# Second feed-forward of a two-layer model: a tile's rows turned by VectorE in 32x32 blocks, after a load in four parts, in place of a turn on TensorE

## The reference

```python
xn = rms_norm(x, norm_scale)
scores = einsum('bsd,ed->bse', xn, w_router)
_, ids = top_k(scores, 2)
c = take_along_axis(softmax(scores), ids)
h = einsum('bsd,ehd->bseh', xn, w_up)
val, gate = split(h, 2)
h = val * silu(gate)
y = einsum('bseh,edh->bsed', h, w_down)
out = sum(take_along_axis(y, ids) * c) + skip
```

## Time and profile before

| | us |
|---|---|
| median of 3 runs | 2190.05 (2188.83 to 2192.83) |
| profiled execution, span from first to last instruction | 2242.6 |
| PE busy over the span | 1743.5 (78%) |
| DVE busy | 1650.1 (74%) |
| ACT busy | 1349.8 (60%) |
| POOL busy | 1185.3 (53%) |

### The profile page before, as it was taken

One profiled execution on the slowest core, in us unless ns is written; L12 is line 12 of the kernel. 1 busy time (PEld: TensorE's weight loads), 2 busy tenths in 40 slices (PEclk: granted clock), 3 DMA queues, 4 the chain that ended last, 5 costly groups with the idle time before them and its releaser, 6 DMA issues. The chain is left out here.

```text
span 2242.6 us, 44681 instructions
## 1 busy us (share of the span) xinstructions
PE 1743.5 (78%) x13783; PEld 1370.5 (61%) x13783; DVE 1650.1 (74%) x4953; ACT 1349.8 (60%) x3266; POOL 1185.3 (53%) x1272
## 2 busy tenths in 40 slices
PE   5688999899976656949994777777777651999994
PEld 5577777777753442426662555555566541999993
DVE  7599999999966982438986999999755432555554
ACT  4577777777744993228772788888444331556551
POOL 3277777877740004842314788888724455444440
PEclk8699999999986756969997999999865555999997
DMA  3000000000013112341200000000220111222217
GB/s 112 12 2 2 2 2 2 2 2 2 2 52 121 39 39 56 48 113 57 66 10 1 1 1 1 1 1 1 78 106 30 34 38 57 70 66 64 66 51 230
DMA packets 103368, 92.05 MB, mean 41 GB/s; under 512 B 11696, under 2 KB 93744, under 8 KB 102432
## 3 DMA queue, kind: packets, MB, share of 16 engines
q1 hardware_dynamic: 80128, 62.77, 9.1%
q0 software_dynamic: 14560, 22.24, 3.8%
q10 hardware_dynamic: 8448, 4.20, 0.6%
HBM read 46.26 MB, written 42.91 MB: 40 GB/s over the span
## 5 line engine op out<-in xcount | busy, mean ns | idle before, releaser
L2263 POOL TENSOR_TENSOR delta_A<-delta_A,delta_sW 128x256 f32<-128x256 f32 x256 | 193.4, 755 | 78.9 <-ACT delta_sW L2110 52.8
L2033 PE MATMUL delta_u<-delta_m,tables_sb 128*128 128x256 f32 x512 | 166.3, 407 | 82.1 <-DVE delta_m L2183 82.1
L2883 POOL DMA_INDIRECT choice_rows<-ffn_y,ffn_xg x135 | 128.7, 953 | 170.8 <-DVE ffn_y L2990 165.6
L644 ACT ACTIVATE attn_p_att<-attn_score,attn_mx 128x224 f32<-128x224 f32 (+7 forms) x512 | 146.6, 394 | 102.3 <-DVE attn_mx L735 102.3
L630 ACT ACTIVATE attn_p_geo<-attn_kp_wide,attn_geo_cols 128x32 f32<-128x32 f32 (+6 forms) x448 | 179.0, 482 | 2.5
L573 PE MATMUL attn_score<-attn_k,attn_q_diag 128*128 128x64 f32 (+5 forms) x1024 | 177.8, 317 | 0.0
L2110 ACT ACTIVATE delta_sW<-delta_W,tables_sb 128x256 f32<-128x256 f32 x256 | 126.6, 506 | 79.6 <-DVE delta_W L2205 75.8
L2033 PEld LDWEIGHTS delta_u<-delta_m,tables_sb 128*128 128x128 f32 x512 | 87.2, 190 | 132.4 <-DVE delta_m L2183 125.7
L2029 PE MATMUL delta_u<-delta_v_own,tables_sb 128*128 128x256 f32 x512 | 153.6, 382 | 9.6 <-DVE xnT L2170 9.6
L2840 POOL DMA_INDIRECT rows<-mix_rows,mix_slot x128 | 124.6, 973 | 56.8 <-issue 52.5
L573 PEld LDWEIGHTS attn_score<-attn_k,attn_q_diag 128*128 128x128 f32 x1024 | 149.5, 193 | 7.3
(11 more groups left out here) (401 smaller groups left out, 5044.8 us busy)
## 6 DMA issues: line engine op xcount, KB each, us to landing
ffn_xg<-rows SPq DMA_DIRECT2D x135, 66.0 KB
acc<-route_zero SPq DMA_DIRECT2D x10, 832.0 KB
comb_rows<-choice_rows SPq DMA_DIRECT2D x32, 256.0 KB
rows<-route_rows SPq DMA_DIRECT2D x8, 640.0 KB, 3.4
load_rows<-in_x SPq DMA_DIRECT2D x16, 256.0 KB, 4.9
bT<-acc SPq DMA_DIRECT2D x16, 256.0 KB, 4.1
qT<-acc SPq DMA_DIRECT2D x16, 256.0 KB, 4.9
x_kept<-xT SPq DMA_DIRECT2D x16, 256.0 KB, 2.1
```

Of the source, the lines that this page charges most:

```text
L644: last = nc.scalar.activation(p_att[:, gr, PAIR_OFF[n]:PAIR_OFF[n] + SLOT * (n + 1)], score[at][:, c:c + SLOT * (n + 1)], ACT.Exp, bias=mx ...
L2033: nc.tensor.matmul(corrections(h, pp % 2), g.t("same_head"), m1[:, h].rearrange("p t d b -> p (t d b)"), start=False, stop=True).then_inc( ...
L2263: nc.gpsimd.tensor_tensor(A[:, t % 8], A[:, (t - 1) % 8], sW[:, t % RING], ALU.add).then_inc(k.A, 1)
L2883: nc.gpsimd.indirect_dma_start(g.choice_rows, bass.IndirectOffsetOnAxis(xg[:, n % RING, D:D + 1].bitcast(U32), 0), y[:, n % RING, :], None ...
```

## The change

SP loads a tile's rows with five transfers. Four bring the channels in four blocks of 32: the transfer for block i puts, for each of the four groups of 32 rows, row b of the group on partition 32 i + b. The fifth brings the last four words of all rows into a tile of its own, `tail`. Then DVE turns within each 32x32 block, and `xgT` has what PE's turn and ACT's copy gave: channel on the partition, row in the free dimension. The turn on PE, its PSUM banks and the copy on ACT are gone. `turn` stands in DVE's list where the loop brings the val weights for tile n+2, ahead of the product of tile n and the weighting of tile n-2. POOL and the weighting read number and share from `tail`.

```diff
+    LOADS = D // SLOT + 1
...
-        xg = s.sb("xg", [128, RING, ROW1])
+        xg = s.sb("xg", [128, RING, D // SLOT, SLOT])
+        tail = s.sb("tail", [128, RING, ROW1 - D])
...
-                sp.dma_start(xg[:, n % RING, :], g.rows1[bass.ds(row, 128), :]).then_inc(ring[n % RING].loaded, 16)
+                here = g.rows1[bass.ds(row, 128), :]
+                by_slot = here[:, 0:D].rearrange("(j b) (i a) -> b i j a", b=SLOT, a=SLOT)
+                for i in range(D // SLOT):
+                    sp.dma_start(xg[SLOT * i:SLOT * i + SLOT, n % RING], by_slot[:, i]).then_inc(ring[n % RING].loaded, 16)
+                sp.dma_start(tail[:, n % RING, :], here[:, D:ROW1]).then_inc(ring[n % RING].loaded, 16)
...
-            def turn(n):
-                par = n % 2
-                pe.wait_ge(ring[n % RING].loaded, 16 * (n // RING + 1))
-                if n >= 2:
-                    pe.wait_ge(k[par].x_copied, n // 2)
-                nc.tensor.transpose(x_ps[par][:, 0:128], xg[:, n % RING, 0:D], g.t("ident")).then_inc(k[par].turned, 1)
-
             def up(n):
                 par = n % 2
-                pe.wait_ge(k[par].x_copied, n // 2 + 1)
+                pe.wait_ge(k[par].turned, n // 2 + 1)
...
-            def copy_x(n):
-                par = n % 2
-                act.wait_ge(k[par].turned, n // 2 + 1)
-                if n >= 4:
-                    act.wait_ge(k[par].val, n // 2 - 1)
-                nc.scalar.activation(xgT[:, n % 4, :], x_ps[par][:, 0:128], ACT.Copy).then_inc(k[par].x_copied, 1)
-
...
+            def turn(n):
+                par = n % 2
+                dve.wait_ge(ring[n % RING].loaded, LOADS * 16 * (n // RING + 1))
+                if n >= 4:
+                    dve.wait_ge(k[par].val, n // 2 - 1)
+                nc.vector.transpose(xgT[:, n % 4, :], xg[:, n % RING].rearrange("p j a -> p (j a)")).then_inc(k[par].turned, 1)
...
             for n in range(AHEAD):
                 bring_val(n)
+                turn(n)
             for n in range(TILES1 + BEHIND):
                 if n + AHEAD < TILES1:
                     bring_val(n + AHEAD)
+                    turn(n + AHEAD)
                 if n < TILES1:
                     hidden(n)
                 if n >= BEHIND:
```

More of the change, by code:

```diff
@@ L2864, in ffn_phase @@
         hid = s.sb("hid", [128, 4, WIDE])
-        x_ps, val_ps, gate_ps, y_ps = ([s.ps(f"{n}{par}") for par in range(2)] for n in ("x", "val", "gate", "y"))
+        val_ps, gate_ps, y_ps = ([s.ps(f"{n}{par}") for par in range(2)] for n in ("val", "gate", "y"))
         ring = [s.sems("loaded sent", n) for n in range(RING)]
         padded = s.sems("padded").padded
-        k = [s.sems("w_val w_gate turned x_copied gate val sg hid down y", par) for par in range(2)]
+        k = [s.sems("w_val w_gate turned gate val sg hid down y", par) for par in range(2)]
         block = s.block()
@@ L2882, in _ @@
                 pool.wait_ge(k[n % 2].y, n // 2 + 1)
-                nc.gpsimd.indirect_dma_start(g.choice_rows, bass.IndirectOffsetOnAxis(xg[:, n % RING, D:D + 1].bitcast(U32), 0),
+                nc.gpsimd.indirect_dma_start(g.choice_rows, bass.IndirectOffsetOnAxis(tail[:, n % RING, 0:1].bitcast(U32), 0),
                                              y[:, n % RING, :], None).then_inc(ring[n % RING].sent, 16)
@@ L2922, in _ @@
             pe.wait_ge(padded, 1)
-            for n in range(AHEAD):
-                turn(n)
             for n in range(TILES1 + BEHIND):
-                if n + AHEAD < TILES1:
-                    turn(n + AHEAD)
                 if n < TILES1:
@@ L2957, in _ @@
                 bring_gate(n)
-                copy_x(n)
             for n in range(TILES1):
@@ L2961, in _ @@
                     bring_gate(n + AHEAD)
-                    copy_x(n + AHEAD)
                 silu(n)
@@ L2989, in output @@
                     dve.wait_ge(ring[n % RING].sent, 16 * (n // RING))
-                nc.vector.tensor_scalar(y[:, n % RING, :], y_ps[par][:, 0:D], xg[:, n % RING, D + 1:D + 2], None, ALU.mult)\
+                nc.vector.tensor_scalar(y[:, n % RING, :], y_ps[par][:, 0:D], tail[:, n % RING, 1:2], None, ALU.mult)\
                     .then_inc(k[par].y, 1)
```

## The result

| | us |
|---|---|
| kernel before, median of 4 runs | 2190.83 (2188.83 to 2192.83) |
| changed kernel, median of 4 runs | 2350.47 (2348.71 to 2351.05) |
| ratio | 1.0727, 95% interval 1.0714 to 1.0740 |
| profiled execution of the changed kernel, span | 2349.2 |

What follows compares the result with a forecast made beforehand. SP's queue was to replace PE as the bound: 135 tiles at 3.40 us, 459 us, put the profiled combine start 171 us later; less profiling overhead, between 2341 and 2361, it took 2348 us, range 2280 to 2405.

Steps and rivals of the forecast that it cites:

- SP's tile, 3.40 us: SP's queue, second feed-forward: row number 0.563 us plus five transfers, 3.40 us a tile, 459 us over 135 tiles.
- the combine's 0.38: Issue time of the combine stage's first load, 0.38 us, taken for each of the four new block transfers instead of 0.34.
- Landing, 2.0 us: End of the second feed-forward: a load is used 2.0 us after its issue starts, the last at 2356.2.
- the last tile, 3.4 us to its weighting: After the last landing at 2356.2, transpose, gate, silu, product and down bring the last tile's weighting to 2359.6.
- The end, 8.54 us: From the last tile's weighting to the combine stage's first issue: 8.54 us, unchanged, so combine starts at 2368.1.
- From trace to median: Unprofiled median lies 52.6 us under the profiled span; SP's 459 us shrink by up to 20, so the change costs 151.
- What was hidden: PE's 15 us of turns, ACT's copies and DVE's transposes in the second feed-forward all lie under SP's queue.
- DVE's 2.06: DVE's cycle for a tile by its own work, with the new transpose of 0.28 us: 2.06 us.
- Packets: DMA engines: 768 packets a tile at 32 ns each, 24.6 us of engine time, 1.5 us a tile over 16 engines.
- the doubling: If read-modify-write doubles the 640 small packets, the DMA engines need 2.8 us a tile, still under SP's 3.40.
- Hidden queue: Faster rival: five transfers take under 2.1 us of SP, DVE's 2.06 rules, 8 us gained, 2182; 4%.
- Clock: Rival: PE, at 59% busy, drops to granted clock 0.5 and is the bound at 3.84 us a tile, 2407; 6%.

Runs made afterwards that it cites:

- the first set of experiments: Kernel before with four plain transfers, 1.0395; changed kernel with all pieces in one transfer, 0.9916, one plain load, 0.9923, or two blocks on ACT, 1.0213.
- the other two sets: Changed kernel with the tail issued by ACT, 1.0432, and kernels turning only some tiles by DVE, 0.9976 to 1.0046, each against the kernel before.
- the mixtures: Kernels with only some tiles loaded by five transfers and turned by DVE, the others as in the kernel before; ratios to that kernel 0.9976 to 1.0046.

## Why the prediction was right, and where it was off

The forecast was 2348, the measurement 2350.47. The mechanism is shown: SP's queue became the bound, and the time moves with the number of transfers on it (5, 4 and 1: 160, 93 and -16 us), with whole rows in four transfers (85 us) as with blocks, and not with the pieces or with DVE. That the number hit within 3 us is luck: the sum of the terms was 171 us where the traces show 157, and I then took 13 us off for a reason that does not exist (158 forecast, 160 measured). By its terms:

- **SP's tile, 3.40 us.** Measured 3.29, and differently made up. The step from one block's transfer to the next is 0.50, not the 0.575 that I had from the combine's 0.38: the issue of a transfer over 32 partitions takes 317 ns, less than the 338 of one over 128, and not more. It is the same without any cut into pieces, 316 ns in the kernel with four transfers of whole rows. An undisturbed tile is then 3.11 us. But 25 of the 675 issues took over 0.44 us, up to 1.66, where the median is 0.32. They bring 0.12 of the 0.18 us by which the mean of 3.29 is longer; the rest are single steps between records of some 0.35 us. I had seen one issue of 1017 ns in the earlier trace rows and left it out of the sum, as it cost nothing while SP had slack. Over 135 tiles: 444 us in place of 459.
- **Landing, 2.0 us, and the last tile, 3.4 us to its weighting.** From the last issue at 2287.05 to DVE's last transpose at 2288.60 it was 1.55, and from there to the last weighting at 2293.82 it was 5.2: the products and downs of two earlier tiles stand between, in lists that I had counted for the last tile alone.
- **The end, 8.54 us.** 8.08. The lines of these two terms:

```profile
2287.05 0.35 SPq L2883 DMA_DIRECT2D ffn_tail<-rows  x1
...
2288.60 0.31 DVE L2967 STREAM_TRANSPOSE ffn_xgT<-ffn_xg 128x128 f32<-128x128 f32 x1 [1.17 <-DMA ffn_tail<-rows]
...
2293.82 0.35 DVE L2983 TENSOR_SCALAR ffn_y<-ffn_y,ffn_tail 128x128 f32<-128x128 f32 x1 [0.80 <-PE ffn_y L2916]
...
2301.90 0.94 SPq L3023 DMA_DIRECT2D comb_rows<-choice_rows  x2
```

  The stage took 458.4 us from the first transfer's preparation to the combine stage (1843.5 to 2301.9) and 301.3 before (1895.6 to 2196.9): 157 where my sum in the trace said 171.
- **From trace to median.** Here I was wrong, and it brought the number back into place. I read the 52.6 us between the profiled span of before and its median as overhead of the profile, and let SP's part shrink by 20. It is no such thing: the changed kernel's profiled span, 2349.2, lies at its median, 2350.47. What was long in the profile of before is the mix stage, which the change doesn't touch. It begins alike and ends 52 us apart; the timeline of SP at its start in both, before:

```profile
1612.37 0.33 SPq L2366 DMA_DIRECT2D mix_w_out<-in_w_out  x1
```

and after:

```profile
1611.09 0.33 SPq L2366 DMA_DIRECT2D mix_w_out<-in_w_out  x1
```

  1612.4 to 1895.6 is 283 us, 1611.1 to 1843.5 is 232. The traces of the first set of experiments have 230 to 234 us there, those of the other two sets 275 to 289, and the kernel before has medians of 2191.98 in the first and of 2242.89 and 2237.40 in the others. So it goes with the set, and each set ran on a chip of its own, not with profiling; chip and hour can't be told apart by these runs, and that the profile of before was taken on such a slower chip is my reading, since the record doesn't name its chip. Each ratio here is within one set. What is slow in the mix stage there was not looked into.
- **What was hidden.** PE's turns, DVE's transpose (311 ns a piece, not 275), ACT's copies: all under SP, as said. With the cover gone (one load) the 15 us of PE came out in full. DVE's 2.06 was a little too much (2.00 in that kernel), since copy, transpose and product follow each other without a gap.
- **Packets.** I had 24.6 us of engine time a tile at 32 ns for each packet. In the changed kernel a share of 0.24 over 3.29 us and 16 engines is 12.6 us for all 768, 16 ns each: small packets are cheaper than large ones, though not in proportion. The Trainium skill (DMA: Bandwidth & Descriptors, Specifications) says that transfers under 512 B are read, modified and written; the doubling that I had considered for it (2.8 us a tile on 16 engines, 45 us of engine time) is not in the 12.6 us.
- **The rivals.** Hidden queue: this was the 4% case, and in the first experiments it is what happens with one or two transfers, so it was right to tie it to about 2.1 us of SP. Clock: it dropped now and then (0.97 and 0.93 in the mean of a window) and never became the bound: PE waited for DVE's transpose, and that for the tail. The Trainium skill (DMA: Bandwidth & Descriptors, Issuing engines are not separate DMA queues) says that the time to start a DMA is "usually small relative to the DMA itself". The trace agrees for one transfer, 0.50 us against a landing of 1.7, and not for the pace of the loop: five issues of 0.50 us each are paid one after the other, while the landings overlap. By the same section of the Trainium skill, issuing from several engines saves only the sequencer's time, and here that was 113 us of the 160.

## What to carry to other kernels

Before a load is cut into more transfers, count what its queue takes per step of the loop: here 0.56 us for a dynamic row number and 0.50 to 0.57 for each transfer (0.50 over 32 partitions, 0.53 for 128 whole rows, 0.57 for 512 pieces over 128 partitions). As long as the sum stays under the bound engine's step the cut is free, small pieces included; from there on each transfer costs its 0.50 us on every step, many times what it was to save. If the gain is on one engine and the cost on another queue, a mixture over the tiles can take some of the gain; but leave the queue a margin over the sum of its undisturbed steps, since it measured 3.29 for 3.11 us in the changed kernel and up to 2.17 for 1.86 in the mixtures.

## What the runs showed that I had not expected

Long issues on SP go with instruction packets on the DMA engines. The changed kernel's stage has 25 issues over 0.44 us; 21 of them start within 0.8 us of a packet of queue q8 (instruction, 16 KB each), the other four beside an 8 KB packet of q14. The DMA view of a stretch with such an issue (packets, MB, and their time as a share of 16 engines):

```profile
q8 instruction: 1, 0.02, 3.0%
```

The next stretch, without one, has no row of q8:

```profile
q1 hardware_dynamic: 585, 0.05, 17.9%
q0 software_dynamic: 33, 0.07, 7.7%
```

The timeline of SP in the first of them (three issues in 2.66 us, undisturbed 1.3):

```profile
1916.34 2.66 SPq L2882 DMA_DIRECT2D ffn_xg<-rows  x3
```

The number of q8 packets hardly differs (25 in the stage before, 24 after; those of q14 go from 25 to 38). The packet alone is not enough: in the kernel with one load 13 of SP's 135 issues start within 0.8 us after such a packet, and none takes over 0.35 us. Nor is it the only companion: with the tail on ACT 52 issues of SP take over 0.44 us, and 20 of them start near one. So the cause stays open; in the changed kernel these issues add 0.12 us to the mean tile.
